# Where the constants of layer 2 are prepared in a fused four-layer graph kernel

## What is computed

```python
x = _layernorm(x + _L0_gnn_ref(x, adj, ...))   # eight Euler steps of a diffusion
x = _layernorm(x + _L1_gnn_ref(x, adj, ...))   # aggregate, two linear maps, two batch norms
x = _layernorm(x + _L2_gnn_ref(x, W, adj))     # masked attention with 4 heads
x = _layernorm(x + _L3_gnn_ref(x, adj, ...))   # graph attention
```

```python
q, k, v = split(h @ W)                          # 4 heads of 32
mask = where(adj == 0, -inf, 0.0)
attn = softmax(q @ k.T / sqrt(32) + mask)
out = attn @ v
```

## Time and profile before

| | us |
|---|---|
| median of 3 runs | 1049.26 |
| lowest and highest | 1047.32 and 1049.3 |
| the profiled execution, its time | 1052.9 |
| the profiled execution, its span | 1050.7 |
| layer 0 to about | 367 |
| layer 1 to about | 479 |
| layer 2 to about | 869 |

### The profile page before, as it was taken

How to read it: one execution, slowest core, us unless ns; L and a number is a source line. 1 busy time by engine, 2 the same in 40 slices (tenths; PEclk the granted TensorE clock), 3 DMA queues, 4 the chain that set the end, 5 groups by cost and what they waited for, 6 DMA issues and landing times. The chain is left out here.

```text
span 1050.7 us, 20959 instructions
## 1 busy us (share of the span) xinstructions
PE 915.6 (87%) x6036; PEld 646.9 (62%) x6036; DVE 651.9 (62%) x2018; ACT 498.0 (47%) x890; POOL 390.1 (37%) x440
## 2 busy tenths in 40 slices
PE   5989999999999589791679999999999965999994
PEld 3779899999998578540344454455445323766673
DVE  4765645554554456562567777777777513889884
ACT  2411312121121045581267777877777534677762
POOL 2110110111110100003246777877777641354454
PEclk9989999999999789996589999999999986999998
DMA  8000000000000000001123342333334300001111
GB/s 225 1 21 11 21 11 22 11 20 10 20 0 0 1 10 0 0 0 28 29 64 86 67 90 65 87 75 75 78 73 91 74 18 4 21 20 30 30 30 30
DMA packets 34217, 40.63 MB, mean 39 GB/s; under 512 B 6656, under 2 KB 17536, under 8 KB 34176
## 3 DMA queue, kind: packets, MB, share of 16 engines
q1 hardware_dynamic: 33072, 40.00, 15.5%
q10 hardware_dynamic: 1104, 0.13, 0.1%
HBM read 6.43 MB, written 4.19 MB: 10 GB/s over the span
## 5 line engine op out<-in xcount | busy, mean ns | idle before, releaser
L1276 DVE CUSTOM_DVE_ANT_0 junk<-bank,mask_ij 128x512 bf16<-128x512 f32 x256 | 166.6, 688 | 82.4 <-PE bank L1356 80.0
L1154 POOL TENSOR_TENSOR half_sum<-prob 128x1024 f32<-128x1024 f32 x64 | 152.1, 2386 | 11.7 <-ACT prob L1217 11.7
L1217 ACT ACTIVATE prob<-wide 128x1024 f32<-128x1024 f32 x128 | 125.3, 1018 | 37.0 <-PE wide L1373 36.2
L380 ACT CAST yT<-wide 128x512 fp32r<-128x512 f32 x48 | 28.2, 588 | 206.3 <-PE wide L696 153.0
L1356 PE MATMUL bank<-qkT 32*128 32x512 f32 x256 | 67.0, 519 | 20.5 <-DVE mx L1276 17.6
L438 POOL TENSOR_TENSOR Xr<-Xf,Xr 128x512 fp32r<-128x512 f32 x16 | 21.5, 1364 | 167.2 <-ACT Xr L375 167.2
L58 PE MATMUL bank<-z,L3T_hi 128*128 128x256 f32 x256 | 73.9, 288 | 7.9 <-DVE z L530 7.9
L152 POOL TENSOR_SCALAR n_rstd<-n_aggr 128x4 f32<-128x4 f32 x32 | 6.5, 204 | 191.0 <-DVE n_aggr L145 179.0
L1369 PE MATMUL wide<-qk_st 128*128 128x512 f32 x256 | 76.6, 421 | 0.7 <-ACT prob L1217 0.3
L1692 PEld LDWEIGHTS bank<-Wh,pr 128*128 128x128 f32 x512 | 61.1, 196 | 23.8 <-issue 19.9
L1692 PE MATMUL bank<-Wh,pr 128*128 128x129 f32 x512 | 65.3, 282 | 10.9 <-ACT pr L1560 10.9
(11 more groups left out here) (280 smaller groups left out, 2305.0 us busy)
## 6 DMA issues: line engine op xcount, KB each, us to landing
qk_st<-qkT SPq DMA_DIRECT2D x192, 128.0 KB, 2.4
out_dram<-rc SPq DMA_DIRECT2D x16, 256.0 KB, 2.3
Xf<-X SPq DMA_DIRECT2D x14, 256.0 KB, 2.3
A<-in_adj_dram SPq DMA_DIRECT2D x4, 256.0 KB, 4.8
qk_st<-neg_row SPq DMA_DIRECT2D x64, 2.0 KB
Xf<-in_x_dram SPq DMA_DIRECT2D x2, 256.0 KB, 6.9
mask_q<-mask_ji SPq DMA_DIRECT2D x16, 32.0 KB, 1.8
w<-in_L_gnn_W_dram SPq DMA_DIRECT2D x2, 128.0 KB, 2.3
```

What stands on the lines that cost most here:

```text
L1154: pool.tensor_tensor(flat(half_sum[h][:]), flat(prob[bp][h][:, 0:2]), flat(prob[bp][h][:, 2:4]), ALU.add).then_inc(h_sum, 1)
L1217: act.activation(flat(prob[bp][h][:, 2 * half:2 * half + 2]), wide[half][:], ACT.Exp, scale=SCALE).then_inc(t_exp, 1)
L1276: dve.tensor_tensor_reduce(out=junk[hh][:], in0=bank[4 + hh][:], in1=m.mask_ij[:, i], scale=1.0, scalar=3.0 * MASKED, op0=ALU.add, op1=ALU ...
```

## The change

The five tensors are now allocated in `layer1` and kept in `m`, so they live through both layers. Their preparation stands in `layer1_first`: the 17 transfers behind the eight that SP issued there, the memsets as GpSimd's only work in that block, and the split of `W` at the end of `weights()` on DVE. SP ends this block only when all transfers have landed. The three waits of PE in layer 2 are gone; the barriers between the blocks take their place.

```diff
     m.O = ctx.enter_context(nc.sbuf_tensor("O", [P, B, N], F32))
...
         @block.sync
...
+            sp.dma_start(m.W2[:], ins["L2_gnn_W"]).then_inc(qkv_in, 16)
+            for j in range(NT):
+                for c in range(4):
+                    sp.dma_start(m.mask_q[32 * j:32 * j + 32, c],
+                                 m.mask_ji[32 * c:32 * c + 32, j]).then_inc(blocks_in, 16)
             sp.wait_ge(w_in, 2 * 16)
             sp.wait_ge(par_in, 6 * 16)
+            sp.wait_ge(qkv_in, 16)
+            sp.wait_ge(blocks_in, 16 * 16)
+
+        @block.gpsimd
+        def _(pool):
+            pool.memset(m.ones_hd[:], 1.0).then_inc(const, 1)
+            for n, (k, end, value) in enumerate(((0, P, 0.0), (1, P, 0.0), (1, 3 * HD + 1, 1.0))):
+                pool.wait_ge(const, n + 1)
+                pool.memset(m.qk_st[3 * HD:end, k].bitcast(F32), value).then_inc(const, 1)
...
                 split(dve, flat(W1T[0][:]), flat(W1T[1][:]), flat(wf[:]), w_hi, 1, w_lo)
+                dve.wait_ge(qkv_in, 16)
+                split(dve, m.Wr[0][:], m.Wr[1][:], m.W2[:, 0:2 * D], qkv_hi, 1, qkv_lo)
...
-            sp.dma_start(W[:], ins["L2_gnn_W"]).then_inc(w_in, 16)
-            for j in range(NT):
-                for c in range(4):
-                    sp.dma_start(mask_q[32 * j:32 * j + 32, c], m.mask_ji[32 * c:32 * c + 32, j]).then_inc(mask_in, 16)
...
-            pool.memset(ones[:], 1.0).then_inc(const, 1)
-            for n, (buf, end, value) in enumerate(((q_st, P, 0.0), (k_st, P, 0.0), (k_st, 3 * HD + 1, 1.0))):
-                pool.wait_ge(const, n + 1)
-                pool.memset(buf[3 * HD:end].bitcast(F32), value).then_inc(const, 1)
-            pool.wait_ge(const, 4)
...
-            dve.wait_ge(w_in, 16)
-            split(dve, Wr[0][:], Wr[1][:], W[:, 0:2 * D], w_hi, 1, w_lo)
...
-            pe.wait_ge(const, 4)
-            pe.wait_ge(w_lo, 1)
-            pe.wait_ge(mask_in, 16 * 16)
```

More of the change, by code:

```diff
@@ L769, in layer1 @@
 def layer1(nc, ctx, m, ins, bank):
+    m.W2 = ctx.enter_context(nc.sbuf_tensor("W", [P, 3 * D], F32))
+    m.Wr = [ctx.enter_context(nc.sbuf_tensor(f"Wr{h}", [P, 2 * D], F32R)) for h in range(2)]
+    m.ones_hd = ctx.enter_context(nc.sbuf_tensor("ones_hd", [P, HD], F32))
+    m.qk_st = ctx.enter_context(nc.sbuf_tensor("qk_st", [P, 2, H, N], F32R))
+    m.mask_q = ctx.enter_context(nc.sbuf_tensor("mask_q", [P, NT, N], BF16))
     m.O = ctx.enter_context(nc.sbuf_tensor("O", [P, B, N], F32))
@@ L811, in layer1_first @@
         h_ps = sem("h_in_psum"); h_sb = sem("h_out"); h_st = sem("h_stats")
+        qkv_in = sem("qkv_w_in"); qkv_hi = sem("qkv_w_high"); qkv_lo = sem("qkv_w_low")
+        blocks_in = sem("mask_blocks_in"); const = sem("rows_set")
         block = own.enter_context(nc.Block())
@@ L1015, in sem @@
             return own.enter_context(nc.semaphore(name))
-        W = sb("W", [P, 3 * D])
-        Wr = [sb(f"Wr{h}", [P, 2 * D], F32R) for h in range(2)]
-        ones = sb("ones_hd", [P, HD])
+        W, Wr, ones, qk_st, mask_q = m.W2, m.Wr, m.ones_hd, m.qk_st, m.mask_q
         Xf = [sb(f"Xb{k}", [P, NT, D]) for k in range(2)]
@@ L1024, in layer2 @@
         Q_LO, Q_HI, K_HI, K_LO = range(4)
-        qk_st = sb("qk_st", [P, 2, H, N], F32R)
         q_st, k_st = qk_st[:, 0], qk_st[:, 1]
@@ L1035, in layer2 @@
         half_sum = [sb(f"half_sum{h}", [P, 2, N]) for h in range(H)]
-        mask_q = sb("mask_q", [P, NT, N], BF16)
         oT = sb("oT", [P, N])
@@ L1045, in layer2 @@
         bn = sem("bn_applied"); b_ps = sem("bn_turned"); res1 = sem("residual1")
-        w_in = sem("w_in"); mask_in = sem("mask_in"); w_hi = sem("w_high"); w_lo = sem("w_low"); const = sem("const")
         x_f = sem("x_in_place")
```

## The result

| | us |
|---|---|
| forecast | 1039.3 (1036.5 to 1042.2) |
| after, median of 20 runs | 1043.70 (1041.1 to 1047.41) |
| before, median of the 20 runs beside them | 1056.45 (1046.96 to 1058.53) |
| ratio after to before | 0.9901, interval 0.9881 to 0.9921 |
| after, the profiled execution, time and span | 1041.16 and 1039.0 |

The ratio is 10.5 us of 1056.45 (8.3 to 12.6), where 9.96 were forecast. The three runs that I had were all of the lower group.

What follows compares the result with a forecast made beforehand. PE, the bound of layer 2's steady part, was held some 10 us at its first turn by constants not yet needed. −9.96 us and three zeros, from the median 1049.26, gave 1039.3 us, range 1036.5 to 1042.2.

Steps and rivals of the forecast that it cites:

- the sum: All terms together: −9.96 us for the wait at layer 2's first turn, and 0 for each of three other terms.
- The zeros of layer 1: Layer 1: the moved transfers, the split and the memsets were each put at cost 0.
- I take no slowing of PE: Layer 1: the mask copies move 0.5 MB while PE aggregates, without slowing it; cost 0.
- The prediction's own sign: Layer 1: first low half of `agT` and first matmul of `W1T` stay at 376.2 and 378.1, counted from the same start.
- The waits that go: Head of layer 2: the first turn, released by `on` alone, starts at 481.35 in place of 491.31, −9.96 us.
- PE's credits: Queue entries of PE before layer 2's first turn: 0 to 0.35 us of cost, taken as 0.
- The transfers in layer 1: SP's queue in layer 1: `W` issued at about 371.7, mask copies landed by 384, cost 0.
- The split and the memsets in layer 1: Layer 1: DVE's split fits an idle time of 2.66 us; memsets slow a cast by 0.07 us; cost 0.
- DVE is blocked: Rival, layer 1: low halves `Xa` wait for GpSimd's memsets, 3.3 us, 1042.6; chance 0.04 together with a late `W`.
- Another clock in the ramp: Rival, early layer 2: a half-clock stretch vanishes (1035.2) or comes once more (1043.4), 4.1 us either way; chance 0.09.
- T held by something else: Rival, layer 2's first turn: barrier, credits or batch norm hide a second lateness, 4.4 us of gain lost, 1043.7; chance 0.03.
- the clock low for long: Rival, layer 2: PE's clock stays at half beyond 541, slower than before, 1051.4; chance 0.02.

Runs made afterwards that it cites:

- mask_only: The kernel after with only the mask copies left in layer 1; W's transfer, its split and the memsets back in layer 2: median 1049.04 us over seven runs.
- mask_stays: The kernel after with the 16 mask copies and PE's wait for them back in layer 2: median 1056.51 us over ten runs, ratio to before 1.0008.
- readers: The kernel before, constants still prepared in layer 2, but the waits moved to their first readers: median 1044.88 us, ratio to before 0.9889.

## Why the prediction was right and wrong

**The step that failed** is the one that puts the sum to a starting value: "so I put the sum to the median: 1049.26 − 9.96". The median of three runs was taken for the kernel's time. It stood for the lower of its two levels, 40 of 92 runs; the mean of all is 1053.5 us, and 1053.5 − 9.9 = 1043.6, where the kernel after has a mean of 1043.8. The page could have warned: the profiled execution was 3.6 us above the median of the three, and three runs of which two agree within 0.04 us say nothing on a second level. I used the spread of the three runs (2 us) as the range's width; the 92 runs before spread over 11.8 us. The range's upper end was also added up wrongly: the highest of the three gives 1049.3 − 9.96 + 0.35 = 1039.7 and not 1041.4. The 1043.7 that were measured lie above both, and above the 1042.2 of the whole range.

That the two means agree within 0.2 us is in part luck. Their standard errors are 0.4 and 0.3 us, so a cost of 0.7 us in layer 1 would not show in them.

**The zeros of layer 1.** A second step failed, with a smaller size. The sum has 0 for everything in layer 1 and "I take no slowing of PE". The prediction's own sign was that the first low half of `agT` and the first matmul of `W1T` stand where they stood. They came 1.44 and 1.50 us later, counted from SP's first issue (9.78 for 8.34 us, 11.75 for 10.25), because PE ran at half clock for 3 us longer. The first block behind them took 0.71 us longer in every trace with the five tensors allocated in layer 1. The first may or may not come from the change, as said above; the second goes with it and had no term.

**The waits that go.** Right: 9.92 us for 9.96. PE's credits cost at most 0.04 us (0.18 us from ACT to PE, 0.14 in the sum). The next steps moved along; the root came 0.22 us behind the aggregate with nothing in its way.

**What stands behind the mask.** The sum had the memsets at 485.71 and the split at 482.6; mask_only measured the first as the next wait, 6.70 us.

**The transfers in layer 1.** Right in their times. `W` was issued at 370.86, 3.90 us behind SP's first issue (3.9 forecast), and the cast began 2.59 us later:

```profile
370.86 0.43 SPq L830 DMA_DIRECT2D W<-in_L_gnn_W_dram  x1
371.34 10.12 SPq L833 DMA_DIRECT2D mask_q<-mask_ji  x16
```

**The split and the memsets in layer 1.** DVE's work held nobody, as forecast, but one of the reasons was wrong. DVE and GpSimd at the head of layer 1, after (before: the earlier trace rows):

```profile
367.14 5.52 POOL L845 MEMSET qk_st<- 32x2048 f32 x3
367.83 1.29 DVE L891 TENSOR_TENSOR Xa<-X,Xa 128x512 fp32r<-128x512 f32 x2 [2.05 <-ACT Xa L856]
...
371.85 0.96 DVE L764 CAST W1T<-wf 128x256 fp32r<-128x256 f32 x1
372.85 0.42 DVE L766 TENSOR_TENSOR W1T<-wf,W1T 128x256 fp32r<-128x256 f32 x1
373.45 0.29 DVE L764 CAST Wr<-W 128x256 fp32r<-128x256 f32 x1 [0.18 <-DMA W<-in_L_gnn_W_dram]
373.78 0.43 DVE L766 TENSOR_TENSOR Wr<-W,Wr 128x256 fp32r<-128x256 f32 x1
376.74 0.69 DVE L897 TENSOR_TENSOR agT<-wide,agT 128x512 fp32r<-128x512 f32 x1 [2.53 <-ACT agT L861]
```

The split ends at 374.21 and the low half `agT` waits for ACT until 376.7, with 2.53 us of idle time. So the split is not what made `agT` late. The rival "DVE is blocked" falls, as the low halves `Xa` took 1.29 us with and without memsets beside them. But the cast of `W1T` took 0.96 us, not 0.29. I had read a price of 0.07 us from the earlier trace rows. That was the wrong size: it was a cast that began shortly before a memset ended. The cast's excess was hidden by the wait for `W` (0.18 us left of it) and by the 2.5 us behind.

**Another clock in the ramp.** I saw the mechanism, but as one stretch of 4 us in the first 60 us of layer 2, with a chance of 0.09, and only for the kernel after. The traces show it in layer 1, layer 2 and layer 3, with some 2 to 3 us in each of three places, and in both kernels; 52 of the 92 runs of before lie at the level that goes with all three. That the work is "the same in the same order" was no argument against it: the unchanged kernel takes either level.

**T held by something else; the clock low for long.** Neither happened: the wait was 2.32 us in four traces, and the slowest of the 32 runs of the kernel after, 1047.44 us, is 0.7 us above the fastest of the 92 of before.

## What to carry to other kernels

A wait at the head of a stage should stand where the data are first read; that alone brought the gain (2.31 us of wait against 12.26), and preparing data one stage earlier only cleared a queue by a further 0.55 us, while layer 1's first block grew by 0.7. What lives longer also moves the other tensors, which is the likely cause of the 0.7 us, so stages whose own work is unchanged belong in the comparison too. When the mask's wait was removed alone, the memsets' wait was next, so look for what is late second before pricing a removal. And a forecast of an absolute time needs the distribution of the runs before: with levels 8 us apart, three runs give the change well (9.92 of 9.96 us in the trace) and the time badly.

## What the runs showed of the hardware

**Levels by the clock.** The same kernel gives runs around 1048.9 and 1057.0 us, with a mean granted clock of 0.942 to 0.949 and 0.932 to 0.937 (in the 72 runs for which it was recorded). That is 114 and 139 us at half clock on average. Had PE been the bound throughout, these 25 us would have cost 12.5 us; the levels are 8 us apart.

**A few ns of each matmul.** With five tensors allocated in an earlier layer, the same aggregation at full clock took 67.6 us for 66.9 (nine traces against five). The allocation is what these kernels share; it was not tried by itself.

**A cast beside a memset.** The cast of a 128x256 tile from SBUF to SBUF ended 0.15 us after the memset beside it: at 372.81 in the kernel after (memsets 367.14 + 5.52 = 372.66), and in mask_stays, where it took 1.17 us, at 372.41 (366.75 + 5.51 = 372.26):

```profile
366.75 5.51 POOL L840 MEMSET qk_st<- 32x2048 f32 x3
...
371.24 1.17 DVE L764 CAST W1T<-wf 128x256 fp32r<-128x256 f32 x1
```

Without memsets it takes 0.29 us (0.30 in mask_only). In readers the cast of `Wr` took 0.55 us and ended at 481.87, while the first of the three memsets, of 1.8 us each, ended at about 481.7. So it seems to wait for the end of the running memset. The subtraction with both inputs in SBUF (0.43 us, and 1.29 for two in `Xa`) is not slowed. The Trainium skill ("GPSIMD Engine Reference", section 1, Specifications) names contention with DVE instructions in a two-port mode or with two SBUF inputs. The traces agree for the cast, with up to 0.9 us, if it ran in a two-port mode, which they don't tell. They don't agree for the two inputs beside a memset, which reads nothing.
